# A conditioned block on one core: the chunk loop written out, the maximum over partitions found by matmuls, and the first tile of x moved forward

## The reference

```python
# layer 0
scale = cond @ norm_w.T + 1.0
ms = jnp.mean(x * x, axis=-1, keepdims=True)
h = x * (scale[:, None, :] * jax.lax.rsqrt(ms + EPS))
u = h @ up_w.T                                   # 512 -> 4096
val, gate = jnp.split(u, 2, axis=-1)
h = val * jax.nn.gelu(gate, approximate=False)
hq = act_quant(h)                                # per row: round(h * 127 / max|h|), scaled back
wq = weight_quant(down_w)                        # round(w / mean|w|), clipped to -1..1, scaled back
x = hq @ wq.T + x                                # 2048 -> 512
# layer 1: its weights depend on the batch
Wd_b = Wd + ((cond @ Wdd.T + bdd) * 0.1).reshape(4, 128, 512)
Wu_b = Wu + ((cond @ Wdu.T + bdu) * 0.1).reshape(4, 512, 128)
x = x + einsum('bln,bdn->bld', relu(einsum('bld,bnd->bln', x, Wd_b) + bd), Wu_b) + bu
```

## Time and profile before

| What | Value |
|---|---|
| Median of 3 runs | 1034.6 us (1031.19 to 1034.74) |
| Profiled execution, own time | 1033.38 us |
| Its span, first to last instruction | 1031.6 us |
| Mean granted TensorE clock | 0.993 |
| PE busy | 966.2 us (94%) |
| DVE busy | 681.9 us (66%) |
| ACT busy | 329.8 us (32%) |
| POOL busy | 51.3 us (5%) |
| Share of the chain that ended last, by engine | PE 74%, DVE 15%, issue 6% |

### The profile page before, as it was taken

How to read it: one execution, slowest core, us unless ns; L and a number is a source line. 1 busy time by engine, 2 the same in 40 slices (tenths; PEclk the granted TensorE clock), 3 DMA queues, 4 the chain that set the end, 5 groups by cost and what they waited for, 6 DMA issues and landing times.

```text
span 1031.6 us, 14604 instructions
## 1 busy us (share of the span) xinstructions
PE 966.2 (94%) x5307; PEld 467.7 (45%) x5307; DVE 681.9 (66%) x1138; ACT 329.8 (32%) x599; POOL 51.3 (5%) x53
## 2 busy tenths in 40 slices
PE   1899999999999989999999899999999999987998
PEld 1555544444444444444444344444444444444454
DVE  1878758766785748766885658756876677428433
ACT  2797832312321222212322223222332222115222
POOL 1000000000000000000000000000000000004153
PEclk9999999999999999999999999999999999989999
DMA  7442341545145412454145412544154512232365
GB/s 275 142 151 88 121 144 62 183 144 163 42 153 152 153 66 85 161 162 145 42 165 164 150 45 92 173 155 133 51 173 155 166 69 82 72 112 82 142 227 182
DMA packets 73314, 134.70 MB, mean 131 GB/s; under 512 B 5268, under 2 KB 10904, under 8 KB 72728
## 3 DMA queue, kind: packets, MB, share of 16 engines
q1 hardware_dynamic: 73240, 133.72, 39.5%
HBM read 112.72 MB, written 20.97 MB: 130 GB/s over the span
## 4 chain that ended last, share of the span: by engine, by line
PE 74%; DVE 15%; issue 6%; ACT 2%; SPq 2%; DMA 1%; DVEq 0%; POOL 0%; ACTq 0%; POOLq 0%
PE bank L892 16%; PE bank L893 16%; PE bank L894 16%; PE bank L950 10%; DVE natT L681 8%; PE bank L905 6%; PE bank L1063 2%; PE bank L1048 2%; DVE h L739 2%; DVE h L660 2%; PE bank L877 1%; PE bank L867 1%; ACT g L516 1%; PE bank L1039 1%; DVE h L833 1%
## 5 line engine op out<-in xcount | busy, mean ns | idle before, releaser
L892 PE MATMUL bank<-x_split,w_hi 128*128 128x512 f16 x1024 | 390.4, 381 | 10.0 <-issue 7.4
L893 PE MATMUL bank<-x_split,w_hi 128*128 128x512 f16 x1024 | 390.0, 381 | 0.0
L894 PE MATMUL bank<-x_split,w_lo 128*128 128x512 f16 x1024 | 389.8, 381 | 0.0
L681 DVE STREAM_TRANSPOSE natT<-nat 128x512 f32<-128x512 f32 x256 | 249.6, 1087 | 1.2 <-PE bank L905 0.8
L516 ACT ACTIVATE g<-h 128x512 f32<-128x512 f32 x128 | 80.6, 630 | 362.3 <-DVE h L739 362.3
L739 DVE SCALAR_TENSOR_TENSOR h<-bank,desc,g 128x512 f32<-128x512 f32 x128 | 94.8, 740 | 106.0 <-issue 66.3
L892 PEld LDWEIGHTS bank<-x_split,w_hi 128*128 128x128 f16 x1024 | 100.7, 98 | 129.9 <-issue 17.3
L894 PEld LDWEIGHTS bank<-x_split,w_lo 128*128 128x128 f16 x1024 | 100.7, 98 | 122.2 <-issue 2.5
L507 ACT ACTIVATE g<-bank,desc 128x512 f32<-128x512 f32 x128 | 87.3, 682 | 208.6 <-PE bank L894 208.6
L893 PEld LDWEIGHTS bank<-x_split,w_hi 128*128 128x128 f16 x1024 | 100.7, 98 | 115.1 <-issue 1.9
L751 DVE TENSOR_TENSOR absrun<-absrun,g 128x512 f32<-128x512 f32 x120 | 83.0, 691 | 75.1 <-ACT g L516 75.1
(11 more groups left out here) (118 smaller groups left out, 543.7 us busy)
## 6 DMA issues: line engine op xcount, KB each, us to landing
nat<-in_L_cond_Wdd SPq DMA_DIRECT2D x64, 512.0 KB, 3.6
nat<-in_L_cond_Wdu SPq DMA_DIRECT2D x64, 512.0 KB, 3.5
qreg<-in_L_cond_up_w SPq DMA_DIRECT2D x32, 256.0 KB, 4.3
xr<-in_x SPq DMA_DIRECT2D x32, 256.0 KB, 4.6
x_scratch<-xr SPq DMA_DIRECT2D x32, 256.0 KB, 4.8
xn<-in_x SPq DMA_DIRECT2D x7, 1024.0 KB, 6.4
out_y<-w_hi SPq DMA_DIRECT2D x7, 1024.0 KB, 4.3
h<-in_L_cond_down_w SPq DMA_DIRECT2D x4, 1024.0 KB, 7.6
```

The costliest lines, as they stand in the source:

```text
L681: last = dve.transpose(natT[:, t, kk, :, :].rearrange("p a (r e) -> p e a r", e=4), nat[:, t, kk, :])
L892: pe.matmul(bank[:, :], w_hi[:, k, cols], xh[:, par, k, :], start=(k == 0), stop=False)
L893: pe.matmul(bank[:, :], w_hi[:, k, cols], xl[:, par, k, :], start=False, stop=False)
L894: mm = pe.matmul(bank[:, :], w_lo[:, k, cols], xh[:, par, k, :], start=False, stop=(k == KD - 1))
```

## The change

Four edits. `chunks` becomes a Python loop, so that each engine's program holds all 8 chunks, and waits compare with constants. The maximum over partitions is made by two small matmuls and two small DVE operations: `absmax` times the identity lays the 128 numbers in one row, DVE takes the maximum of the row and places it in a 1 x 1 tile, and a product with a row of ones spreads it over the 128 partitions. `partition_all_reduce` is gone. On DVE the scaling of x and of the first pair of weights goes ahead of the chain that ends in `sc`. The first pair's `w_hi` and `w_lo` go ahead of `x_hi` and `x_lo`, and the first gate tile waits for `ta_freed` per step of k.

```diff
@@ names
-            return (TA, GATE[0], VAL[0], HY)[k] if isinstance(c, int) and c < 0 else TA
+            return (GATE[0], TA, VAL[0], HY)[k] if c < 0 else TA
@@ chunks
-        def chunks(eng, run):
-            run(0, 0, 0, 0)
-            with eng.Fori(0, NCH // 2 - 1) as i:
-                run(2 * i + 1, 1, i + 1, i)
-                run(2 * i + 2, 0, i + 1, i)
-            run(NCH - 1, 1, None, NCH // 2 - 1)
+        def chunks(run):
+            for c in range(NCH):
+                run(c, c % 2, (c + 1) // 2 if c + 1 < NCH else None, max(c - 1, 0) // 2)
@@ gpsimd
-            pool.wait_ge(setup_dve, 3)
-            pool.partition_all_reduce(allmax[:, :], absmax[:, :], P, RMAX).then_inc(setup_pool, 1)
             norm_x(0)
@@ scalar
+            w_hi_half(0)
             for k in range(KD):
                 x_hi(-1, 0, k)
-            w_hi_half(0)
             w_square(2)
@@ vector
-            dve.wait_ge(setup_pool, 1)
-            dve.tensor_scalar(allmax[:, :], allmax[:, :], 2.0 ** -100, 2.0 ** 126, ALU.max, ALU.min).then_inc(setup_dve, 1)
+            dve.wait_ge(max_turned, 1)
+            dve.tensor_reduce(max_row[:, :], VAL[1][0:1, 0:P], AX.X, ALU.max).then_inc(max_found, 1)
+            dve.wait_ge(max_found, 1)
+            dve.tensor_scalar(max_diag[:, :], identf[0:1, 0:1], max_row[:, 0:1], None, ALU.mult).then_inc(max_found, 1)
+            dve.wait_ge(x_rstd, 1)
+            for t in range(TT):
+                dve.tensor_scalar(xn[:, t, :], xn[:, t, :], rstd[:, t:t + 1], None, ALU.mult).then_inc(x_scaled, 1)
+            w_exponents(0)
+            w_scale(0)
+            dve.wait_ge(max_spread, 1)
+            dve.tensor_scalar(allmax[:, :], VAL[1][:, P:P + 1], 2.0 ** -100, 2.0 ** 126, ALU.max, ALU.min).then_inc(setup_dve, 1)
...
             dve.tensor_scalar(sc[:, :, :], sc[:, :, :], inv2[:, 0:1], 2.0 ** X_BITS, ALU.mult, ALU.mult).then_inc(setup_dve, 1)
-            dve.wait_ge(x_rstd, 1)
-            for t in range(TT):
-                dve.tensor_scalar(xn[:, t, :], xn[:, t, :], rstd[:, t:t + 1], None, ALU.mult).then_inc(x_scaled, 1)
-            w_exponents(0)
-            w_scale(0)
             dve.wait_ge(setup_dve, 9)
             dve.tensor_copy(sc_now[:, :], sc[:, :, 0]).then_inc(sc_copied, 1)
+            w_lo_half(0)
             for k in range(KD):
                 x_lo(-1, 0, k)
-            w_lo_half(0)
@@ tensor
                     if jj == 1:
-                        pe.wait_ge(setup_dve, 1)
+                        pe.wait_ge(setup_dve, 4)
...
-            def up_products(par, ft, bank, done):
+            def up_products(par, ft, bank, done, x_waits=False):
                 cols = slice(ft * P, (ft + 1) * P)
                 for k in range(KD):
+                    if x_waits:
+                        pe.wait_ge(ta_freed, k + 1)
...
-                if first:
-                    pe.wait_ge(ta_freed, KD)
-                else:
+                if not first:
                     pe.wait_ge(h_done, FT * c - 1)
...
-                    up_products(par, FT + j, GATE[j % 2], gate_full)
+                    up_products(par, FT + j, GATE[j % 2], gate_full, first and j == 0)
...
+            pe.wait_ge(setup_dve, 3)
+            pe.wait_ge(consts_ready, 3)
+            pe.matmul(VAL[1][0:1, 0:P], absmax[:, :], identf[:, :], start=True, stop=True).then_inc(max_turned, 1)
+            pe.wait_ge(max_found, 2)
+            pe.matmul(VAL[1][:, P:P + 1], ones[0:1, :], max_diag[:, :], start=True, stop=True).then_inc(max_spread, 1)
             for t in range(TT):
                 pe.wait_ge(x_scaled, t + 1)
```

More of the change, by code:

```diff
@@ L12 @@
 AX = mybir.AxisListType
-RMAX = bass.bass_isa.ReduceOp.max
 P = 128
@@ L91, in conditioned_block @@
         allmax = sb("allmax", [P, 1], F32)
+        max_diag = sb("max_diag", [1, 1], F32)
+        max_row = sb("max_row", [1, 1], F32)
         pow2 = sb("pow2", [P, 1], F32)
@@ L156, in conditioned_block @@
         small_in, base_in, cond_in = sem("small_in"), sem("base_in"), sem("cond_in")
-        setup_pe, setup_act, setup_dve, setup_pool = (sem(n) for n in ("setup_pe", "setup_act", "setup_dve", "setup_pool"))
+        setup_pe, setup_act, setup_dve = (sem(n) for n in ("setup_pe", "setup_act", "setup_dve"))
+        max_turned, max_found, max_spread = sem("max_turned"), sem("max_found"), sem("max_spread")
         desc_done, cond_spread, cond_turned, cond_copied, cond_ready, sc_copied = (sem(n) for n in ("desc_done", "cond_spread", "cond_turned", "cond_copied", "cond_ready", "sc_copied"))
@@ L211, in is_first @@
         def is_first(c):
-            return isinstance(c, int) and c == 0
+            return c == 0
         def ta_x(c, k):
-            if isinstance(c, int) and c < 0:
+            if c < 0:
                 return k
@@ L377, in _ @@
             load_x(1)
-            chunks(sp, run)
+            chunks(run)
             c = NCH - 1
@@ L425, in run @@
                     norm_x(c + 1)
-            pool.wait_ge(setup_dve, 3)
-            pool.partition_all_reduce(allmax[:, :], absmax[:, :], P, RMAX).then_inc(setup_pool, 1)
             norm_x(0)
-            chunks(pool, run)
+            chunks(run)
             pool.wait_ge(bu_in, 16)
@@ L548, in _ @@
             w_square(1)
+            w_hi_half(0)
             for k in range(KD):
                 x_hi(-1, 0, k)
-            w_hi_half(0)
             w_square(2)
             w_hi_half(1)
-            chunks(act, run)
+            chunks(run)
             def copy_x1(c, par, slices=range(KD)):
-                if not (isinstance(c, int) and c < 2) and 0 in slices:
+                if not (c < 2) and 0 in slices:
                     act.wait_ge(down_full, c - 1)
@@ L565, in relu_down @@
                 act.wait_ge(down_full, c + 1)
-                if not (isinstance(c, int) and c < 2):
+                if not (c < 2):
                     act.wait_ge(up_full, TT * (c - 1))
@@ L820, in _ @@
                 dve.tensor_copy(cond_diag[q4, :, NB * r:NB * r + NB], cond4[q4, :, :]).then_inc(cond_ready, 1)
-            chunks(dve, run)
+            chunks(run)
             def add_up(c, par, tiles=range(TT)):
@@ L873, in turn_x @@
                     pe.wait_ge(x_scaled, TT * (n + 1))
-                if not (isinstance(u, int) and u < KD):
+                if not (u < KD):
                     pe.wait_ge(ta_freed, u)
@@ L926, in turn_absrun @@
                 pe.wait_ge(max_done, FT * (c + 1))
-                if isinstance(c, int) and c == NCH - 1:
+                if c == NCH - 1:
                     pe.wait_ge(layers_ready, 2 * NB)
@@ L1026, in _ @@
             turn_w(0)
-            chunks(pe, run)
+            chunks(run)
             def turn_x1(c, b, par, slices=range(KD)):
@@ L1058, in up_layer @@
                         pe.wait_ge(up_done, TT * c)
-                    if t == 2 and not (isinstance(c, int) and c < 2):
+                    if t == 2 and not (c < 2):
                         pe.wait_ge(y_done, TT * NCH)
```

## The result

The changed kernel took 1010.09 us in the median of 4 runs (1008.49 to 1011.17), the kernel before 1033.94 us beside it (1031.19 to 1034.74). The ratio is 0.9771, with a 95% interval of 0.9751 to 0.9792: 23.8 us faster. Forecast were 1011 us. The profiled execution took 1011.17 us; its span is 1009.1 us, at a mean granted clock of 0.994.

What follows compares the result with a forecast made beforehand. PE was taken as the bound, busy 966.2 of 1031.6 us, so only ending its idle pays. Loop 10.6 and setup 12.2 sum to 22.8 us; 1033.4 less that is 1010.6, forecast as 1011, range 1006 to 1019.

Steps and rivals of the forecast that it cites:

- The loop: Chunks 1 to 6 written out: two taken branches' idle on PE (7.4 us) and the slow clock behind (3.2) go, 10.6 us.
- The register work: Register instructions of the loop's waits, on every engine: costed at nothing since covered; if not, a gain of at most 2 us.
- POOL: the step: Setup: without the reduction and the configuration behind it, POOL's first power starts at 8.32 instead of 22.80 us.
- the rival that the silence belongs to the first power in any case: POOL's 11.66 silent us come behind the mean squares anyway; setup gains only 2.2 us, total 1020.6; chance 0.1.
- T: Start of DVE's scaling of x in the setup: from 23.88 to 9.45 us, 14.4 us earlier.
- From T to the second tile: Setup, from DVE's scaling of x to PE's second tile: 13.45 us, against 12.88 before, with DVE's scaled weights as bound.
- "worth nothing" for the new order: Setup: the first tile's earlier start gains nothing, since PE then waits for DVE's scaling of the second and third weight pairs.
- The clock in the first tile: PE's first tile may run at the slow clock: counted as nothing, bound 1.5 us, up to 3 if it lasts.
- Chunk 1's x: Its load lands between 26.4 and 31.0 us, taken as 28.7; ACT waits 1.6 us, all counted on the path.
- Sum: Whole kernel: loop 10.6 plus setup 12.2 make 22.8 us, giving 1010.6 from the profiled 1033.4 us.
- Setup: Start of the kernel through chunk 1's x load: 13.8 us gained less 1.6 of waiting, net 12.2, bounds 9.9 and 13.8.
- One rival: Written-out chunks: instructions arrive late throughout, 5.3 us a stall, slower from the sixth on, 1053 us for eight; chance 0.03.

Runs made afterwards that it cites:

- the first experiment: The changed kernel with chunks 1 to 6 put back in the hardware loop, the setup as changed: 1021.23 us, ratio 0.9875.
- the experiment on chunk 1's x: The changed kernel with the fourth pair of up weights and chunk 1's x loaded ahead of the last down weights on SP: 1009.83 us, ratio 0.9753.
- the filler: The changed kernel with 9 unread identity transposes on PE between the first eight weight transposes and the first tile: 1009.39 us, one run.

## Why the prediction was right

**The loop: 10.6 us forecast, 10.7 in the trace.** Idle and clock came as worked out, and came back with the branch alone (the first experiment). The register work, which I had bounded by 2 us, is hardly to be seen: chunks 1 and 3, which held no branch, took 112.26 and 112.30 us before and 112.12 and 112.16 now. The queue of instructions did not become a cost either: 42 packets, and no idle without a releaser. The Trainium skill (Runtime: NRT & Kernel Launch, Instruction fetch mechanics) says that a long program need not fit, and this trace agrees.

**POOL: the step was right.** I had the power waiting for its configuration, with 0.1 for the rival that the silence belongs to the first power in any case. The power runs 0.16 us behind its input in the changed kernel; with an unused reduction the silence returns, and it stands behind a memset that itself runs at once. Shown is that the reduction ahead of the power causes it; which instruction of the change back spends the time is not.

**T: 9.45 forecast, 10.76 measured, the term that was mis-sized most.** I took the mean squares' end from the kernel before, 8.32; it was 9.54. ACT squared the last tile of x from 8.62 on, because the last of the first four loads landed at 8.6, against 7.1 before (the last issue and the longest time to landing). In the seven other kernels in which the power is free and DVE scales x first, T was 9.87 to 10.65. The first loads' landing thus moves T by a microsecond, which the earlier trace rows as a single execution could not show; before, it was hidden behind POOL. T moved by 13.1 us and not 14.4.

**From T to the second tile: 13.45 forecast, 12.91 measured.** The bound was the one named: DVE's scaled weights (they end at 22.86, T + 12.1; forecast T + 13.0), and not PE's first tile. The half microsecond too much goes with the eight transposes ahead, which I took at 1.92 us from the kernel before and which took 1.04; where they did take 1.91 us, in the experiment on chunk 1's x, the scaling ended at T + 13.2 and the second tile stood at T + 13.8. But "worth nothing" for the new order was right only against the kernel before, whose first tile had the full clock. In the three kernels with the old order and a slow first tile the second is at T + 15.1 to T + 15.8. One of these is the kernel before with the memset, whose power is late, so a slow first tile does not need the early power.

**The clock in the first tile: counted as nothing, and it fell.** I had bounded it at 1.5 us net, up to 3; the tile took 1.52 us longer. It cost 0.15 us, since DVE's scaling hid it, as the filler showed. The Trainium skill (TensorE: Matmul & The Clock Gate, Part 1), by whose rule the sparse first tile is the place for the slow clock, was right on the clock here, as the 0.62 shows, though with x loaded first the same tile ran at 1.00; and the time that I worked out from it was not lost.

**Chunk 1's x: landing forecast at 28.7, measured 28.95; the wait 1.6 forecast, 1.04 measured.** ACT asked 0.8 us later than I had it, by the later T. On the path it was worth 0.9, so counting the whole wait was right. That the landing came so near is luck: I had taken the middle between 26.4 and 31.0, and neither way of working it out was shown right. Issued into the busy queue, the load took 12.05 us, against at most 8.8 us before.

**Sum.** Setup 12.2 forecast; 12.8 at the end of chunk 0, of which 0.6 is a wait for the scales of the down weights at 135.36 that vanished and that I had not counted. The tail gave back 1.1 us, which I had not foreseen either. 22.8 forecast, 22.5 between the spans: T was 1.3 too early and the tail cost 1.1, while the distance behind T (0.5), the load (0.7), the scales (0.6) and the chunks (10.8 against 10.6) came out better than forecast. The mechanism of each step held; that the total is nearer than its parts is luck.

One rival was summed wrongly. At 5.3 us a stall, five make 26.5 us, so the kernel would have been slower than before from the fifth on, and not from the sixth; nothing of it came.

## What to carry to other kernels

An idle on an engine with no releaser, next to an instruction that configures it or to a taken branch, is a cost of the program and not of the data: look for what the program holds there, and whether another engine can do the small job. When a wait of many microseconds goes, what was hidden under it (the first loads' landing, the next load, the clock) can come to matter by a microsecond or so each; list these before summing. Where one engine is always late by the same small amount, move what consumes it some products down the order: that was worth 20.8 us here, by the medians and with the order of loads changed too (by itself 0.3 us, within the noise), nearly as much as the whole change.

## What the runs showed of the hardware

- Changing POOL over to the reduction took 7.7 to 8.0 us in five kernels, and back to the power 10.1 to 11.7 us in the four in which it was not hidden; a memset in between ran 0.25 us behind the reduction's start. Each cost stands ahead of the first instruction of the other kind, however long its input has been there, and behind a MODIFY_POOL_CONFIG whose own record is 0.01 or 0.08 us. Another such instruction, at L412 of the kernel before, was followed by its operation within 0.1 us, so not each of them costs this.
- The same branch, taken by five engines, cost only PE: 4.343 and 5.157 us, on the others at most 0.063 us. In the four kernels that keep the loop it took 3.96 to 5.34 us on PE, with idles of 2.9 to 4.3 us ahead of the next product. No kernel without the loop had an idle of PE without a releaser over 0.2 us there.
- The granted clock in the first tile does not follow from the order. In the changed kernel, with 2.32 us of idle ahead of it, the mean was 0.62; with work in the gap it was 1.00; with x loaded first it was 1.00 too, after 2.23 us of idle. What goes with it is the time of the eight transposes ahead of the idle. In the five kernels without filler in which they took 1.04 to 1.11 us the tile began at the lower level (means 0.50 to 0.62). In the five in which they took 1.91 or 1.92 us it began at 2.4 GHz, and in four of these it kept it (1.00). In the two with 1.81 and 1.82 us the mean was 0.61. What decides between the two is open.
